# Attention of a fused layer: TensorE adds the negative maximum to four heads by an identity product, and scores are issued one tile pair ahead

## The reference, cut to what matters

```python
q = (queries @ Wq + bq).reshape(N, L, H, D)      # N = 16 batches, L = 64, H = 16 heads, D = 16
k = (keys @ Wk + bk).reshape(N, S, H, D)         # S = 1601 context positions
v = (values @ Wv + bv).reshape(N, S, H, D)
sm = jnp.einsum('nlhd,nshd->nlhs', q, k) / math.sqrt(D)
sm = jax.nn.softmax(sm, axis=1)
attn = jnp.einsum('nlhs,nshd->nlhd', sm, v).reshape(N, L, H * D)
return attn @ Wo + bo
```

## Time and profile before

| what | value |
|---|---|
| median of 3 runs | 1523.06 us (1522.17 to 1528.12) |
| span of the profiled execution, first to last instruction | 1519.6 us |
| TensorE busy over the span | 1339.1 us (88%) |
| VectorE busy | 1291.7 us (85%) |
| ScalarE busy | 1163.9 us (77%) |
| GpSimd busy | 1107.2 us (73%) |

### The profile page before, as it was taken

One profiled execution on the slowest core, in us unless ns is written; L12 is line 12 of the kernel. 1 busy time (PEld: TensorE's weight loads), 2 busy tenths in 40 slices (PEclk: granted clock), 3 DMA queues, 4 the chain that ended last, 5 costly groups with the idle time before them and its releaser, 6 DMA issues. The chain is left out here.

```text
span 1519.6 us, 34485 instructions
## 1 busy us (share of the span) xinstructions
PE 1339.1 (88%) x12560; PEld 1001.5 (66%) x12560; DVE 1291.7 (85%) x1894; ACT 1163.9 (77%) x2975; POOL 1107.2 (73%) x1092
## 2 busy tenths in 40 slices
PE   5999999999999999978777777777777899999995
PEld 5888888888888888755333333333333678888884
DVE  4899999999999999987699999999999645666664
ACT  5888888888888888754699999999999235555552
POOL 2988888888888888754299999999999351443431
PEclk9999999999999999999899999999999999999998
DMA  4223131111111111005654110200000026888994
GB/s 135 59 74 103 45 85 49 39 46 38 46 44 38 48 42 31 2 2 132 163 89 80 17 32 1 35 14 1 2 1 1 1 68 261 311 303 308 307 310 139
DMA packets 106866, 132.99 MB, mean 88 GB/s; under 512 B 43274, under 2 KB 97617, under 8 KB 103256
## 3 DMA queue, kind: packets, MB, share of 16 engines
q1 hardware_dynamic: 96872, 61.61, 16.7%
q0 software_dynamic: 9840, 69.36, 12.8%
HBM read 110.47 MB, written 14.49 MB: 82 GB/s over the span
## 5 line engine op out<-in xcount | busy, mean ns | idle before, releaser
L565 POOL TENSOR_TENSOR half<-prob 128x512 f32<-128x512 f32 (+1 forms) x208 | 266.9, 1283 | 91.8 <-ACT prob L602 89.4
L597 ACT ACTIVATE prob<-ps_s,mx 128x64 f32<-128x64 f32 (+1 forms) x1040 | 239.1, 339 | 98.5 <-DVE prob L708 98.5
L1372 DVE TENSOR_TENSOR state<-ps_u,state 128x1024 f32<-128x1024 f32 x252 | 297.3, 1219 | 7.1 <-POOL state L1235 3.1
L701 DVE TENSOR_REDUCE mx<-ps_s 128x16 f32<-128x1024 f32 (+1 forms) x208 | 253.0, 1216 | 13.8 <-PE ps_s L648 12.3
L1330 PE MATMUL ps_y<-state,cz 128*32 128x256 f32 x2048 | 247.8, 384 | 1.8 <-DVE zs L1352 1.0
L648 PE MATMUL ps_s<-qbd,kT 64*128 64x256 f32 (+1 forms) x1664 | 221.1, 395 | 14.7 <-ACT prob L597 12.7
L708 DVE TENSOR_TENSOR prob<-ps_s,mx 128x192 f32<-128x192 f32 (+3 forms) x416 | 198.4, 518 | 7.2
L648 PEld LDWEIGHTS ps_s<-qbd,kT 64*128 64x128 f32 (+1 forms) x1664 | 147.8, 182 | 67.1 <-issue 38.5
L1330 PEld LDWEIGHTS ps_y<-state,cz 128*32 128x32 f32 x2048 | 109.1, 110 | 106.3 <-issue 30.0
L1312 PE MATMUL ps_u<-x_rows,b_diag 48*128 48x256 bf16 x1024 | 79.4, 275 | 112.0 <-DVE state L1372 105.0
L602 ACT ACTIVATE prob<-prob 128x704 f32<-128x704 f32 (+1 forms) x208 | 173.8, 836 | 0.0
(11 more groups left out here) (263 smaller groups left out, 3413.2 us busy)
## 6 DMA issues: line engine op xcount, KB each, us to landing
raw<-in_ctxT_dram SPq DMA_DIRECT2D x80, 268.0 KB, 2.8
x_rows<-ssm_x SPq DMA_DIRECT2D x96, 64.0 KB
raw<-in_ctxT_dram SPq DMA_DIRECT2D x16, 261.0 KB, 2.8
b_diag<-blank SPq DMA_DIRECT2D x2, 2048.0 KB, 8.9
slot_rows<-blank SPq DMA_DIRECT2D x1, 3483.0 KB, 15.4
xg<-slot_rows SPq DMA_DIRECT2D x27, 128.0 KB, 4.9
ssm_x<-xp SPq DMA_DIRECT2D x6, 384.0 KB, 3.9
back<-y_slots SPq DMA_DIRECT2D x8, 256.0 KB, 4.5
```

The lines of the kernel that those rows point to most:

```text
L565: pool.tensor_tensor(half[0:rows, :, :], prob[0:rows, g % SLOTS, :, 0:L // 2], prob[0:rows, g % SLOTS, :, L // 2:L], ALU.add).then_inc(hal ...
L597: ins = nc.scalar.activation(prob[0:rows, g % SLOTS, h, :], part[:, h, :], ACT.Exp, bias=mx[0:rows, g % 2, h:h + 1])
L701: nc.vector.tensor_reduce(mx[0:rows, g % 2, :], part, AX_X, ALU.max, negate=True)\
L1372: nc.vector.tensor_tensor(h, flat(ps_u[k % 2][:, :, :]), h, ALU.add).then_inc(state_ready, 1)
```

## The change

Of the 16 heads of a tile, VectorE now subtracts the maximum for heads 0 to 7 only, in one instruction. For heads 8 to 11 TensorE does it: shift(g), one fp32r product with the identity as weights and mx, repeated 64 times along each of the four heads, as the moving operand, accumulates onto the scores in the second bank. ScalarE takes exp of heads 12 to 15 one by one as before, then of heads 8 to 11 from PSUM in one instruction without a bias, then of the 512 elements that VectorE wrote. mx is stored as fp32r, and an fp32r copy of the identity, ident_r, is made by GpSimd in the start-up.

The order on TensorE changes: scores(0) and scores(1) stand ahead of the loop, and pair i is shift(2i), the first half of the jobs, values(i-1), shift(2i+1), scores(2i+2), the second half of the jobs, the outputs, scores(2i+3). ScalarE takes the second half of the jobs behind its second tile. The first scores product in a bank has start set, the second one (c = 1) no longer; z_ready takes over what rz_ready counted.

```diff
@@ attention
-        mx = sbuf("mx", [P, 2, H])
+        mx = sbuf("mx", [P, 2, H], F32R)
...
@@ exponential(g), ScalarE
-                act.wait_ge(sub_ready, 2 * g + 1)
+                act.wait_ge(max_ready, g + 1)
+                act.wait_ge(shifted, g + 1)
+                if g >= SLOTS:
+                    act.wait_ge(pv_done, g - SLOTS + 1)
...
-                for h in range(H - DIRECT, H):
-                    ins = nc.scalar.activation(prob[0:rows, g % SLOTS, h, :], part[:, h, :], ACT.Exp,
-                                               bias=mx[0:rows, g % 2, h:h + 1])
-                ins.then_inc(direct_done, 1)
-                act.wait_ge(sub_ready, 2 * g + 2)
-                rest = prob[0:rows, g % SLOTS, 0:H - DIRECT, :]
+                for h in DIRECT:
+                    nc.scalar.activation(prob[0:rows, g % SLOTS, h, :], part[:, h, :], ACT.Exp,
+                                         bias=minus_max[0:rows, g % 2, h:h + 1])
+                nc.scalar.activation(prob[0:rows, g % SLOTS, SHIFTED, :], part[:, SHIFTED, :], ACT.Exp)\
+                    .then_inc(direct_done, 1)
+                act.wait_ge(sub_ready, g + 1)
+                rest = prob[0:rows, g % SLOTS, 0:HC, :]
                 nc.scalar.activation(rest, rest, ACT.Exp).then_inc(exp_ready, 1)
@@ TensorE
-                    pe.wait_ge(sub_ready, 2 * g - 2)
+                    pe.wait_ge(sub_ready, g - 1)
...
-                                               start=True, stop=True, skip_group_check=True)
+                                               start=(c == 0), stop=True, skip_group_check=True)
...
+            def shift(g):
+                rows = tile(g)[2]
+                heads = SHIFTED.stop - SHIFTED.start
+                pe.wait_ge(max_ready, g + 1)
+                nc.tensor.matmul(ps_s[g % 2][0:rows, 1, 0:heads * L], sb["ident_r"][0:rows, 0:rows],
+                                 mx[0:rows, g % 2, SHIFTED].unsqueeze(2).broadcast_to([rows, heads, L]),
+                                 start=False, stop=True, skip_group_check=True).then_inc(shifted, 1)
...
+            scores(0)
+            scores(1)
             for i in range(PAIRS + 3):
+                first, second = halves(jobs_of(i))
                 if i < PAIRS:
-                    scores(2 * i)
-                    scores(2 * i + 1)
-                    for kind, n, j in jobs_of(i):
-                        job(m, kind, n, j)
-                        m += 1
+                    shift(2 * i)
+                for kind, n, j in first:
+                    job(m, kind, n, j)
+                    m += 1
                 if 1 <= i <= PAIRS:
                     values(i - 1)
+                if i < PAIRS:
+                    shift(2 * i + 1)
+                if i + 1 < PAIRS:
+                    scores(2 * i + 2)
+                for kind, n, j in second:
+                    job(m, kind, n, j)
+                    m += 1
                 for g in outputs_of(i):
                     outputs(g)
+                if i + 1 < PAIRS:
+                    scores(2 * i + 3)
@@ VectorE
-                for heads in (slice(H // 2, H - DIRECT), slice(0, H // 2)):
-                    nc.vector.tensor_tensor(prob[0:rows, g % SLOTS, heads, :], part[:, heads, :],
-                                            mx[0:rows, g % 2, heads].unsqueeze(2)
-                                            .broadcast_to([rows, heads.stop - heads.start, L]), ALU.add).then_inc(sub_ready, 1)
+                nc.vector.tensor_tensor(prob[0:rows, g % SLOTS, 0:HC, :], part[:, 0:HC, :],
+                                        minus_max[0:rows, g % 2, 0:HC].unsqueeze(2).broadcast_to([rows, HC, L]), ALU.add)\
+                    .then_inc(sub_ready, 1)
```

More of the change, by code:

```diff
@@ L43 @@
 SLOTS = 8
-DIRECT = 5
+SHIFTED = slice(8, 12)
+DIRECT = range(12, 16)
 DI, NS, NH, HD = 512, 64, 8, 64
@@ L148, in _ @@
                                       fill=0.0, base=DH - 1, pattern=[[DH, HC]], channel_multiplier=-1))
+            c.link(pool.tensor_copy(sb["ident_r"][:, :], sb["ident"][:, :]))
             for part in a["ctxh"] + a["ctxl"]:
@@ L204, in _ @@
             pe.wait_ge(w_low, 1)
-            pe.wait_ge(masks_made, 11)
+            pe.wait_ge(masks_made, 12)
             for j in range(2):
@@ L463, in attention @@
         z_ready = sem("z_ready")
-        rz_ready = sem("rz_ready")
+        shifted = sem("a_shifted")
         vn_ready = sem("vn_ready")
@@ L469, in attention @@
         block = ctx.enter_context(nc.Block())
+        minus_max = mx[:, :, :].bitcast(F32)
+        Z_STEPS = 3
         TILES = NB * NT
@@ L492, in jobs_of, with halves @@
             return found + [("q", n, m) for n in range(1, TOK // TQ) if 13 * n + 2 == i for m in range(KD)]
+        def halves(jobs):
+            return jobs[0:len(jobs) // 2], jobs[len(jobs) // 2:]
         def last_pair(n, c):
@@ L568, in _ @@
                 if g // 2 >= 2:
-                    pool.wait_ge(z_ready, g // 2 - 1)
+                    pool.wait_ge(z_ready, Z_STEPS * (g // 2 - 2) + 1)
                 pool.tensor_tensor(quarter[0:rows, g // 2 % 2, g % 2, :, :], half[0:rows, :, 0:L // 4],
@@ L715, in scale_values @@
                 nc.vector.tensor_reduce(z[:, :, :], quarter[:, p % 2, :, :, :], AX_X, ALU.add).then_inc(z_ready, 1)
-                dve.wait_ge(z_ready, p + 1)
+                dve.wait_ge(z_ready, Z_STEPS * p + 1)
                 for e in range(2):
                     nc.vector.reciprocal(rz[:, e, :].rearrange("p (c j h) -> p j c h", c=KD, h=HG),
-                                         z[:, e, :].rearrange("p (j c h) -> p j c h", c=KD, h=HG)).then_inc(rz_ready, 1)
-                dve.wait_ge(rz_ready, 2 * p + 2)
+                                         z[:, e, :].rearrange("p (j c h) -> p j c h", c=KD, h=HG)).then_inc(z_ready, 1)
+                dve.wait_ge(z_ready, Z_STEPS * (p + 1))
                 dve.wait_ge(v_product, p + 1)
@@ L2129, in perceiver_layer @@
               "hmask": sbuf("hmask", [P, HC]), "qmask": sbuf("qmask", [P, KD * HQ]),
-              "gmask": sbuf("gmask", [P, HG]),
+              "gmask": sbuf("gmask", [P, HG]), "ident_r": sbuf("ident_r", [P, P], F32R),
               "minus_half": sbuf("minus_half", [P, TT]), "blank": sbuf("blank", [P, D + 2])}
```

## The result

The changed kernel takes 1549.85 us (median of 4 runs, 1547.42 to 1550.35) against 1522.62 us, a ratio of 1.0176 with a 95% interval of 1.0159 to 1.0193: 27 us slower, where 38 were forecast. The profiled execution took 1547.42 us with a span of 1545.7.

What follows compares the result with a forecast made beforehand. TensorE was taken to bound pairs with keys after the change: 601.2 + 21.7 (three query pairs) + 60.9 (eleven without jobs) = 683.8 us against 645.3, 38.5 more. That gave 1561.5 us, forecast range 1548 to 1578 (chance 0.50).

Steps and rivals of the forecast that it cites:

- The bound: Attention pairs before: TensorE needs 6.02 us with keys, VectorE 6.08; after the change TensorE alone is the bound there.
- The pair: TensorE's pair with keys: 6.02 plus two shifts 0.24, scores to full array 0.31, shift to scores 0.11, making 6.68 us.
- Scores to keys: TensorE's step from scores to key products: a gap of 0.21 plus a first key product 0.10 longer, together 0.31 us.
- The reason for 0.11: Step from second shift into scores, not in the trace: taken at 0.11 us because leaving scores costs most in the rows.
- The pair of 6.88: TensorE's pair if the step from shift to scores is priced like scores to keys, 0.31; left as a rival.
- The laid-out pair: Schedule over 6.68 us: second maximum ready at 1.25, its shift reached at 2.37, 1.1 us to spare; nothing late.
- 90 x 6.68: Term of the attention's sum: 90 pairs with keys at 6.68 us each, 601.2 us.
- No change: New changes of array form cost nothing, only the shifts' 0.24 is added: 6.26 a pair, 1522.5 us; chance 0.08.
- faster: Shifts run inside drains and new gaps are free, TensorE keeps 6.02 us a pair: 1500 us; chance 0.06.
- dear changes or late weights: Shift to scores at 0.31 gives 1580 us; each shift at 0.39 as well, up to 1630; chance 0.20.
- a wait: TensorE idles at the shift if maxima come over 1.1 us late; 0.3 us a pair gives 1590; chance 0.02.
- Cheap changes: TensorE hides part of the second gap: 0.24 and half of 0.42 give 6.47 a pair, 1542 us; chance 0.14.

Runs made afterwards that it cites:

- e4: Kernel before with its own order: VectorE subtracts heads 0 to 7 only, ScalarE takes heads 8 to 11 without their maximum, no shift; 1503.86 us.
- e8: Kernel before, no shift: heads 8 to 15 share one maximum, ScalarE takes them in one instruction, VectorE subtracts for heads 0 to 7 only; 1499.47 us.
- e9: Kernel before with one maximum for all 16 heads: VectorE subtracts nothing, ScalarE takes 1024 elements in one instruction; 1488.69 us.
- e3: Changed kernel with its order but no shift product, the maximum not subtracted for heads 8 to 11; 1533.13 us.
- e5: Changed kernel with each shift product issued twice, so heads 8 to 11 are lowered by twice their maximum; 1572.53 us.

## Why the prediction was right

- **The number.** 1561.5 was forecast and 1549.85 measured, in the lower corner of the forecast's 1548 to 1578. The mechanism held in its terms, but one reason and one term did not.
- **The bound.** Right: TensorE 500.00 of 500 us, VectorE's idle time ended by it. Its own need, 6.02 by the rows before, is the floor with the order of the kernel before: e4, e8 and e9 take ever more work from the other engines and all stop at 6.05.
- **The pair.** Forecast 6.68, measured 6.65. Two shifts at 0.12: e3 (6.44 against 6.65) and e5 (6.88) give 0.21 and 0.23 for two. Scores to keys 0.31: 1.07 - 0.86 + 0.23 - 0.12 = 0.32. From the full array into scores, taken at 0.11 from neighbours: 0.08.
- **The reason for 0.11.** Wrong, though the number was close: "what costs most is to leave scores". Record by record, leaving for the full array costs 0.20 and entering from it 0.18. The prediction's 0.31 already held the 0.10 of the longer first couple of scores, so 0.31 and 0.11 add up to the right total with the wrong shares.
- **The rule on changes of tiling mode.** The trace has a gap at all five changes, of 0.08 to 0.11, whichever way. In "TensorEngine Tiling (Array Packing)", Key Properties, the Trainium skill says only that there is a drain, and that agrees. The pair of 6.88 failed by its price, not because the changes differ in kind: 0.31 is 0.20 for leaving and 0.10 of the entry, so charged for both new steps it makes 0.62, where the two cost 0.39 together.
- **VectorE.** Right: 5.42 forecast, 5.43 measured in pairs without jobs.
- **Waits.** Right: 2.3 us in total for maxima. The laid-out pair had 1.1 us to spare; in the trace the second shift starts 1.0 behind the end of its maximum (403.75 + 1.23 to 406.00).
- **The sum.** Too high: 38.5 forecast, 30.4 in the attention (to tile 206), 27.2 in the medians. The term that was mis-sized is "90 x 6.68". It charged a whole pair from the first on, but the first pair has no values and the first two no outputs: three pairs took 16.34 us (33.13 to 49.47), not 20.0, so 3.7. The before side of the sum was measured, its start included; the after side was not. The other 4 to 5 are in pairs: a mean of 6.63, not 6.68, over the pairs with keys, and some 0.25 rather than 0.54 more for a pair with query products. From the attention's 30.4 to the profile's 26.1 it is plus 1.0 for the later start (33.13 for 32.11) and minus 5.4 behind the last sum z (835.1 us of span left for 840.5), which the change doesn't touch; over the profiles taken here that rest lies between 835 and 844 us. It is not explained further.
- **The rivals.** "No change" and "faster" fell with the new gaps; "dear changes or late weights" with the records and e5; "a wait" with the view of waits. "Cheap changes" (6.47) isn't the cause of the smaller loss, as the pair is 6.65.

## What to carry to other kernels

Before work goes to another engine, lay out that engine's own need for one round, gaps included; here VectorE was busy 97% and TensorE 99%, and 0.53 us off the one was paid with 0.63 on the other. On TensorE, count how often the form of the array changes in a round (64-row halves, full, 32 columns): two more changes cost 0.39 us, two whole products 0.21 to 0.23. When a stretch is priced by distances, look at its first record apart, or a cost of entering is booked as one of leaving. Look for work that vanishes (a shared maximum) before work that moves, and compare like with like: a forecast round times its count has no start-up, a measured stretch has.

## What the runs showed of the hardware

- A change of form leaves a gap of 0.08 to 0.11 us, whichever form is left or entered: full array to scores (64-row halves) 0.08, scores to full array 0.10, full array or scores to 32-column outputs 0.09 to 0.10, outputs to scores 0.11. Behind it the first product is 0.10 longer in scores and on the full array and 0.02 in outputs. These are medians over all records of the changed kernel between 60 and 690 us.
- Going from fp32 to fp32r products on the full array leaves no gap: 0.98 us are four records of 0.216 and one of 0.118.
- A moving operand that repeats one value 64 times runs at the same speed as plain data: 0.11 to 0.12 us for 256 columns in fp32r.
